# Third attention with its biased rows kept from the first load, and the first feed-forward with base on VectorE and its variance moved up

## The reference, cut to what matters

```python
def head(W, b):
    e = jnp.einsum('bmc,hc->bmh', x, W) + b
    q, k, v = jnp.split(e, 3, axis=1)
    attn = jax.nn.softmax(jnp.einsum('bmd,bnd->bmn', q, k) * SCALE, axis=-1)
    return jnp.einsum('bmn,bnd->bmd', attn, v)
outs = jax.vmap(head)(W_embed, b_embed)
qkv = jnp.concatenate([outs[i] for i in range(outs.shape[0])], axis=1)
out = jnp.einsum('bmd,cd->bmc', qkv, W_out) + b_out
return out + x        # x is _layernorm(h); the caller adds h
```

## Time and profile before

| | us |
|---|---|
| median of the runs shown | 4401.44 |
| the profiled execution | 4401.72 |
| its span | 4399.9 |
| first feed-forward, from its first sum to its last output add | 632.9 to 853.0 |
| third attention, from its first centering to its last output add | 2120.3 to 2409.4 |
| busy over the span: PE, VectorE, ScalarE, GpSimd | 3833.5, 2827.1, 2353.6, 1993.0 |

### The profile page before, as it was taken

One profiled execution on the slowest core, in us unless ns is written; L12 is line 12 of the kernel. 1 busy time (PEld: TensorE's weight loads), 2 busy tenths in 40 slices (PEclk: granted clock), 3 DMA queues, 4 the chain that ended last, 5 costly groups with the idle time before them and its releaser, 6 DMA issues.

```text
span 4399.9 us, 111398 instructions
## 1 busy us (share of the span) xinstructions
PE 3833.5 (87%) x31697; PEld 2615.2 (59%) x31697; DVE 2827.1 (64%) x9320; ACT 2353.6 (53%) x5933; POOL 1993.0 (45%) x2308
## 2 busy tenths in 40 slices
PE   7488857698999799999776769999999999899999
PEld 7355533386666566666665546666666666555555
DVE  2577735585788644444444778888888888455554
ACT  5455524322444344444333547888888888555555
POOL 0144327674666412222454655555555555434333
PEclk9999966697999899999655779999999999899999
DMA  2111123331111333333111220000000000233332
GB/s 53 36 31 31 27 39 100 82 83 41 38 38 36 72 75 77 77 77 79 38 42 44 65 61 10 11 11 11 11 11 11 11 13 17 63 77 76 77 77 56
DMA packets 483268, 207.06 MB, mean 47 GB/s; under 512 B 452850, under 2 KB 473326, under 8 KB 482930
## 3 DMA queue, kind: packets, MB, share of 16 engines
q1 hardware_dynamic: 483058, 204.73, 20.5%
HBM read 158.75 MB, written 45.91 MB: 47 GB/s over the span
## 4 chain that ended last, share of the span: by engine, by line
PE 48%; issue 19%; POOL 15%; DVE 8%; SPq 6%; DMA 2%; ACT 1%; POOLq 0%; DVEq 0%; ACTq 0%
POOL att_P L3588 8%; PE sw_pH L4192 5%; PE moe_pH L2727 5%; PE sw_pY L4179 4%; PE moe_pY L2750 4%; PE att_pS L982 3%; DVE att_M L1177 3%; PE moe_pH L2731 2%; PE moe_pH L2737 2%; POOL att_norm_rstd L673 1%; SPq L2894 1%; PE att_pS L2220 1%; PE att_pO L1044 1%; SPq L2888 1%; PE ret_pR L1837 1%
## 5 line engine op out<-in xcount | busy, mean ns | idle before, releaser
L3588 POOL TENSOR_TENSOR att_P<-att_P,att_rden 125x498 f32<-125x498 f32 x512 | 520.4, 1017 | 510.2 <-DVE att_rden L3883 509.6
L3776 ACT ACTIVATE att_P<-att_Z,att_nb 125x249 f32<-125x249 f32 x1024 | 504.1, 497 | 22.8 <-DVE att_nb L3895 21.3
L2792 DVE TENSOR_TENSOR moe_hT<-moe_silu,moe_pH 128x498 f32<-128x498 f32 x384 | 258.8, 674 | 310.5 <-ACT moe_silu L2776 310.5
L4240 ACT ACTIVATE sw_hT<-sw_pH,sw_b 128x498 f32<-128x498 f32 x512 | 319.0, 675 | 219.7 <-PE sw_pH L4192 219.7
L3697 PEld LDWEIGHTS att_pP<-att_ident,att_P 124*125 124x125 f32 (+1 forms) x2048 | 262.5, 187 | 234.0 <-issue 234.0
L3697 PE MATMUL att_pP<-att_ident,att_P 124*125 124x124 f32 (+1 forms) x2048 | 349.6, 293 | 50.6 <-issue 28.8
L3895 DVE CUSTOM_DVE_ANT_0 att_Z<-att_pS,att_mask 125x249 f32<-125x249 f32 x1024 | 365.8, 412 | 29.3 <-PE att_pS L3685 27.3
L2776 ACT ACTIVATE moe_silu<-moe_pH 128x498 f32<-128x498 f32 x384 | 225.5, 587 | 261.6 <-PE moe_pH L2731 175.9
L3783 ACT ACTIVATE att_PTr<-att_pP 125x498 f32<-125x498 f32 x512 | 297.5, 581 | 100.0 <-PE att_pP L3697 90.9
L2703 POOL TENSOR_TENSOR moe_xe<-moe_share,moe_x 128x1992 f32<-128x1992 f32 x32 | 130.0, 4063 | 428.4 <-DMA moe_share<-mixing 402.1
L4099 POOL TENSOR_TENSOR sw_acc<-sw_acc,sw_Z 128x249 f32<-128x249 f32 x224 | 154.1, 688 | 364.6 <-DVE sw_Z L4319 363.9
(11 more groups left out here) (463 smaller groups left out, 9691.9 us busy)
## 6 DMA issues: line engine op xcount, KB each, us to landing
moe_share<-mixing SPq DMA_DIRECT2D x64, 498.0 KB, 6.1
sw_share<-mixing SPq DMA_DIRECT2D x64, 498.0 KB, 6.1
ffn_W<-in_ffn_pairs SPq DMA_DIRECT2D x64, 192.0 KB, 2.4
att_F<-h_stream SPq DMA_DIRECT2D x192, 62.5 KB
att_X<-h_stream SPq DMA_DIRECT2D x192, 62.5 KB
h_stream<-att_H SPq DMA_DIRECT2D x64, 62.5 KB
ffn_F<-h_stream SPq DMA_DIRECT2D x64, 62.5 KB
ret_F<-h_stream SPq DMA_DIRECT2D x64, 62.5 KB
```

Source lines behind the costliest of these rows:

```text
L3588: g.tensor_tensor(own, own, bc(rden[:, j % 2, c, :], T), ALU.mult).then_inc(*scaled.one())
L3776: ins = a.activation(P[:, r, c, t, :], Z[:, r, c, t, :], ACT.Exp, scale=-1.0, bias=nb[:, r, c, t:t + 1], accum_out=den[:, r, c, t:t + 1])
L4240: a.activation(hT[:, k % 4, :, :], pH[:, place, :, 0:T], ACT.Relu, bias=b1[:, k:k + 1]).then_inc(*hid_ready.one())
```

## The change

**Third attention.** `keep`, X and its semaphore go: SP's loop now issues `ahead` for pair n+6 and `store` for pair n. The add with bias moves from the pair's fifth part to its second, right behind centering, reads F and writes base, which now has six buffers; it waits for the output add of the pair six before. `ahead` waits for this add instead of for centering. Everything that had two buffers keeps two (u % 2), and the loop body has six slots.

**First feed-forward.** base moves from GpSimd's step 2 to VectorE's step 2, behind the product with gamma; VectorE's product with rstd now also waits for the output add of earlier pairs. The tail's variance moves from VectorE's step 3 to step 2, so that it stands ahead of acc and H1.

```diff
--- stage_ffn0, GpSimd
             def last(n, u, step):
                 if step == 0:
                     g.wait_ge(*t_variance.after(n))
                     g.tensor_tensor(trstd[:, :], tvar[:, :], norm.expo[:, :], ALU.pow).then_inc(*t_powered.one())
-                if step == 2:
-                    g.wait_ge(*h_ready.before(n))
-                    g.tensor_tensor(base[:, :, :], g4(Fi[:, u, :, :, :]), bcm(beta[:, :], 1, 4),
-                                    ALU.add).then_inc(*base_ready.one())
--- stage_ffn0, VectorE
             def ends(n, u, step):
-                if step == 3:
+                if step == 2:
                     v.wait_ge(*t_squared.after(n))
...
             def last(n, u, step):
                 if step == 1:
                     v.wait_ge(*t_powered.after(n))
+                    v.wait_ge(*h_ready.before(n))
...
                 if step == 2:
...
+                    v.tensor_tensor(base[:, :, :], g4(Fi[:, u, :, :, :]), bcm(beta[:, :], 1, 4),
+                                    ALU.add).then_inc(*base_ready.one())
--- stage_attention2
-    STEPS, WAVES, ROUNDS = 5, 8, 8
+    STEPS, PERIOD, WAVES, ROUNDS = 5, 6, 14, 8
...
-        X = st.sb("X", [TH, 2, HEADS, 2, C])
...
-        base = st.sb("base", [TH, 2, HEADS, 2, C])
+        base = st.sb("base", [TH, PERIOD, HEADS, 2, C])
...
         def ahead(sp, n, u):
-            sp.wait_ge(*norm.centered.lagging(n))
+            sp.wait_ge(*biased.lagging(n))
...
-        def keep(sp, n, u):
-            sp.wait_ge(*base_ready.lagging(n))
-            st.held(sp)
-            for j, r, src in parts(h, n):
-                sp.dma_start(X[r, u, j, :, :], src).then_inc(*kept.one(u))
...
                     n = j * 2 + u
-                    keep(sp, n + 2, u)
                     ahead(sp, n + 6, u)
                     store(sp, n, u)
             for n in range(PAIRS - 6, PAIRS - 2):
-                keep(sp, n + 2, n % 2)
                 store(sp, n, n % 2)
--- stage_attention2, GpSimd
             def even(n, u, step):
                 if step == 3:
                     g.wait_ge(*xn_ready.before(n))
-                    norm.center(g, n, g4(F[:, u, :, :, :]))
+                    norm.center(g, n, g4(F[:, u % 2, :, :, :]))
+                    if since(n, PERIOD):
+                        g.wait_ge(*h_ready.after(n - PERIOD))
+                        st.held(g)
+                    g.tensor_tensor(base[:, u, :, :, :], F[:, u % 2, :, :, :], bias[:, :, :, :], ALU.add).then_inc(
+                        *biased.one())
...
             def soft(n, u, step):
                 own = base[:, u, :, :, :]
                 if step == 0:
-                    if since(n, 2):
-                        g.wait_ge(*h_ready.after(n - 2))
-                    g.wait_ge(*kept.after(n, u))
-                    g.tensor_tensor(own, X[:, u, :, :, :], bias[:, :, :, :], ALU.add).then_inc(*biased.one())
-                if step == 1:
                     g.wait_ge(*biased.after(n))
                     g.wait_ge(*xn_ready.after(n))
-                    g.tensor_tensor(own, own, xn[:, u, :, :, :], ALU.add).then_inc(*base_ready.one())
-            waves(g, (nothing, even, turn_in, nothing, soft, nothing), STEPS)
+                    g.tensor_tensor(own, own, xn[:, u % 2, :, :, :], ALU.add).then_inc(*base_ready.one())
+            waves(g, (nothing, even, turn_in, nothing, soft, nothing), STEPS, PERIOD)
```

More of the change, by code:

```diff
@@ L2908, in _ @@
                 ahead(sp, n, n)
-                keep(sp, n, n)
         yield
@@ L2950, in turn_in @@
                         g.wait_ge(*xT_done.after(n - 2))
-                    norm.scale(g, n, g4(xn[:, u, :, :, :])).then_inc(*xn_ready.one())
+                    norm.scale(g, n, g4(xn[:, u % 2, :, :, :])).then_inc(*xn_ready.one())
             def soft(n, u, step):
@@ L3011, in proj @@
                     for hd in range(HEADS):
-                        ins = pe.matmul(pA[:, hd * TH:(hd + 1) * TH], G[:, hd, :], xT[:, u, 0:TH], start=True,
+                        ins = pe.matmul(pA[:, hd * TH:(hd + 1) * TH], G[:, hd, :], xT[:, u % 2, 0:TH], start=True,
                                         stop=True)
@@ L3018, in proj @@
                         r = slice(b * C, (b + 1) * C)
-                        ins = pe.matmul(pV[:, b, 0:HEADS * C], xT[r, u, 2 * TH:T], wv[r, :], start=True, stop=True)
+                        ins = pe.matmul(pV[:, b, 0:HEADS * C], xT[r, u % 2, 2 * TH:T], wv[r, :], start=True, stop=True)
                     ins.then_inc(*v_done.one())
@@ L3029, in soft @@
                             r = slice(b * C, (b + 1) * C)
-                            ins = pe.matmul(pS[:, b, hd * TH:(hd + 1) * TH], AT[r, u, hd, :],
-                                            xT[r, u, TH:2 * TH], start=True, stop=True)
+                            ins = pe.matmul(pS[:, b, hd * TH:(hd + 1) * TH], AT[r, u % 2, hd, :],
+                                            xT[r, u % 2, TH:2 * TH], start=True, stop=True)
                     ins.then_inc(*s_done.one())
@@ L3051, in ends @@
                             ins = pe.matmul(pO[:, at:at + C], PTr[:, g * TH:(g + 1) * TH],
-                                            V[:, u, b, hd * C:(hd + 1) * C], start=True, stop=True)
+                                            V[:, u % 2, b, hd * C:(hd + 1) * C], start=True, stop=True)
                     ins.then_inc(*o_done.one())
-            waves(pe, (nothing, nothing, turn_in, proj, soft, ends), STEPS)
+            waves(pe, (nothing, nothing, turn_in, proj, soft, ends), STEPS, PERIOD)
         @block.scalar
@@ L3068, in turn_in @@
                     a.wait_ge(*xT_done.after(n))
-                    a.activation(xT[:, u, :], pX[:, 0:T], ACT.Copy).then_inc(*xT_ready.one())
+                    a.activation(xT[:, u % 2, :], pX[:, 0:T], ACT.Copy).then_inc(*xT_ready.one())
             def proj(n, u, step):
@@ L3075, in proj @@
                         a.wait_ge(*o_done.after(n - 2))
-                    a.activation(V[:, u, :, :], pV[:, :, 0:HEADS * C], ACT.Copy).then_inc(*v_ready.one())
+                    a.activation(V[:, u % 2, :, :], pV[:, :, 0:HEADS * C], ACT.Copy).then_inc(*v_ready.one())
             def soft(n, u, step):
@@ L3086, in soft @@
                             g = b * HEADS + hd
-                            ins = a.activation(P[:, u, g, :], pS[:, b, hd * TH:(hd + 1) * TH], ACT.Exp,
-                                               bias=nb[:, g:g + 1], accum_out=den[:, u, hd, b:b + 1])
+                            ins = a.activation(P[:, u % 2, g, :], pS[:, b, hd * TH:(hd + 1) * TH], ACT.Exp,
+                                               bias=nb[:, g:g + 1], accum_out=den[:, u % 2, hd, b:b + 1])
                     ins.then_inc(*exp_ready.one())
-            waves(a, (nothing, even, turn_in, proj, soft, nothing), STEPS)
+            waves(a, (nothing, even, turn_in, proj, soft, nothing), STEPS, PERIOD)
         @block.vector
@@ L3114, in pre @@
                 if step == 4:
-                    v.wait_ge(*loaded.after(n, u))
+                    v.wait_ge(*loaded.after(n, u % 2))
                     v.wait_ge(*norm.centered.before(n))
-                    norm.sums(v, n, g4(F[:, u, :, :, :]))
+                    norm.sums(v, n, g4(F[:, u % 2, :, :, :]))
             def turn_in(n, u, step):
@@ L3143, in ends @@
                     v.wait_ge(*o_ready.before(n))
-                    v.reciprocal(rden[:, :], den[:, u, :, :].rearrange("p n b -> p (n b)")).then_inc(
+                    v.reciprocal(rden[:, :], den[:, u % 2, :, :].rearrange("p n b -> p (n b)")).then_inc(
                         *den_ready.one())
@@ L3153, in ends @@
                     v.wait_ge(*base_ready.after(n))
-                    v.wait_ge(*stored.lagging(n, u))
+                    v.wait_ge(*stored.lagging(n, u % 2))
                     st.held(v)
-                    v.tensor_tensor(g4(H1[:, u, :, :, :]), tmp[:, :, :], g4(base[:, u, :, :, :]),
+                    v.tensor_tensor(g4(H1[:, u % 2, :, :, :]), tmp[:, :, :], g4(base[:, u, :, :, :]),
                                     ALU.add).then_inc(*h_ready.one())
-            waves(v, (pre, nothing, turn_in, proj, soft, ends), STEPS)
+            waves(v, (pre, nothing, turn_in, proj, soft, ends), STEPS, PERIOD)
         yield
```

7 lines of the change are left out of this document (3 added, 4 removed).

## The result

The changed kernel took 4319.44 us in the median of four runs (4316.81 to 4323.29), the kernel before 4401.63 beside it (4396.05 to 4402.95): a ratio of 0.9821, 95% interval 0.9809 to 0.9833. The forecast was 4323, with a range of 4302 to 4354. The two profiled executions differ by 84.9 us of span.

A forecast was written before the change was run, and what follows sets the result against it. SP's issue was taken to bound the third attention, a ring of GpSimd and VectorE the first feed-forward. Terms -61.8 + 0.8 - 17.8 = -78.8 us from 4401.7 gave 4323 us, range 4302 to 4354.

The forecast's parts named there:

- SP's issue sets the slot before: Third attention: SP's three groups of six issues cost 9.04 us a slot; without second loads, about 6.2.
- PE comes next at 6.57, at a clock of 0.50: Third attention: with nothing late, PE takes 6.57 us per pair at the 1.2 GHz level, the slot's lower end.
- the first rival: Third attention: PE gets its full 2.4 GHz clock, SP's 6.2 a slot bounds, 76.7 us gained, 4308 us; chance 0.08.
- the ring over two slots of 13.52: Third attention: chain from scores' transposes through VectorE and ScalarE to the next, 6.76 us a slot; 6.75 taken, 61.8 us gained.
- The first add moved, 0.8 us in the filling slots: Third attention: the moved add frees its buffer 0.99 us later, delaying loads once while filling: 0.8 us lost (0 to 1.5).
- Six slots a loop body, nothing: Third attention: four loop passes instead of thirteen; fewer returns gain nothing, or up to 3 us, left out.
- rival 4: Third attention: returns of the larger loop body wait for code, making the kernel slower, 4443 us at 40 us each; chance 0.02.
- First feed-forward, 5.9 a slot: First feed-forward: slot falls from 6.56 to 5.9 us, between two PE and ScalarE values, 5.66 and 6.05: 17.8 us gained.
- the ring from centering over the squares and the variance to `acc` and the coming variance: First feed-forward: longer ring through VectorE and GpSimd, 4.9 us with hand-offs, up to 6.1 with delayed tiny scalings.
- Base on VectorE at 0.43, in a gap: First feed-forward: base takes about 0.43 us on VectorE where it waits for the tail's squares; GpSimd loses 0.74 of 5.44.
- the second rival: Both stages: VectorE and GpSimd lock each other out, 7.8 and 7.3 us a slot, 4389 us; chance 0.03 at full size.
- Variance ahead, the wait of 1.13 goes: First feed-forward: tail's variance no longer behind the output add, so power follows centering and GpSimd's 1.13 us wait goes.

The follow-up runs named there:

- e_sp6: The changed kernel with the six second loads per pair issued by SP again, into a buffer nobody reads or waits for: 4378.4 us.
- e_sp1: The changed kernel with the second load's bytes per pair moved in one DMA on SP, read by nobody: 4330.3 us.
- e_pe: The changed kernel with two of three heads' matmuls into pA left out in the third attention's loop: 4313.8 us, one run.
- e_att: The kernel before with only the third attention's part of the change, first feed-forward as before: 4355.8 us, ratio 0.9903.
- e_base: The kernel before with only the feed-forward's base add moved to VectorE, tail's variance left behind the output add: 4361.5 us, ratio 0.9922.
- e_pad: The kernel before with the third attention's part of the change and 17 one-column memsets on VectorE at that stage's head: 4340.5 us, ratio 0.9864.
- again_best: The changed kernel with the tail's variance left behind the output add, repeat timing on one chip with the change: 4312.8 us, ratio 0.9794.
- e_first: The changed kernel with the tail's variance left behind the output add and base put ahead of VectorE's two scalings: 4307.6 us, ratio 0.9787.
- again_after: The changed kernel itself, timed once more: 4319.8 us, ratio 0.9818.

## Why the prediction held, and where it didn't

- **SP's issue sets the slot before**: right, shown by `e_sp6` and `e_sp1`. The estimate was that 12 issues cost 6.2 a slot; they cost 6.32 in `e_pe`.
- **PE comes next at 6.57, at a clock of 0.50**: right; 17 of 27 slots are at that floor, and the first rival, the full clock once PE's pauses are gone, didn't come: 0.50 with PE busy for 99.7% of 170 us. The step that failed is the ring over two slots of 13.52, from which 6.75 was taken. VectorE's output add did get slower, as feared (0.92 us in the mean between 2130 and 2320, before 0.74 between 2160 and 2390), but PE hardly ever waits for that chain, and `e_pe` runs at 6.32 with the same VectorE and GpSimd work (though less of PE's, of which the ring holds a part), so in the change the ring doesn't set the slot. It was read in a stretch in which PE itself was full, and so probably counted waits for PE as work of the ring. Mis-sized by 27 x 0.11 = 3 us. The full slots gave 244.06 - 179.28 = 64.8 us; some 2.4 of them were lost at the stage's head (last section), so the stage as a whole gained 62.5.
- **The first add moved, 0.8 us in the filling slots**: not seen. First to fifth transposes took 23.29 us before and 23.23 after. Its own cost was hidden.
- **Six slots a loop body, nothing**: right in that stage. But the changed program moved another stage's loop, a cost that no step of the prediction had: rival 4 looked for a wait for code at the returns of the changed loop, and VectorE's pauses came in a stage behind, 25.2 us in `e_att`. In the change they are 14 of 0.44 us, and the fourth attention took 1163.0 us instead of 1158.7. That they are waits for code is argued, not shown.
- **First feed-forward, 5.9 a slot**: the gain was under-sized (26.8 us instead of 17.8), and the step behind the number is the one that failed. The 5.9 was taken between two values of a path through PE and ScalarE, 5.66 and 6.05. In the change that path doesn't set the slot, which is 5.60 at a high clock and 5.66 at the low one. The clock of the stage also rose, from 0.64 to 0.73 (windows, 660 to 820), so the long hidden-layer groups of 2.03 were not the rule. What holds is the ring from centering over the squares and the variance to `acc` and the coming variance. The prediction had it, at 4.9 to 6.1, but as the shorter one. PE does come in where the variance is last: at the low clock `e_base` takes 5.87.
- **Base on VectorE at 0.43, in a gap**: wrong where GpSimd works on whole rows, 0.83 (27 of 32 pairs in the change); right beside its powers, 0.42 (31 of 32 at most 0.42 in `e_base`). The rule weighed in the prediction, that the two engines lock each other out (the Trainium skill, SBUF — State Buffer, Who interferes with whom), agrees with the first. It doesn't give the second by itself, as the power reads SBUF too, four values a row. And the 0.69 that the prediction put beside the rule is a scaling with one tensor as input, not two. Full-size locks, the second rival, didn't come.
- **Variance ahead, the wait of 1.13 goes**: it went, and moved to the power of the coming pair as predicted (17.0 us, 27 times, from 660 to 820). With base alone it goes only where PE's clock is high (0.14 in the good slots, some 0.9 to 1.1 in most of the long ones), and yet `e_base` is faster in the mean. The prediction took both edits as one gain. It listed what stands behind the variance in its new place, but not that `acc` need not wait for the squares if the variance stays where it was.
- **Tail slots at nothing**: 26.8 us in the stage, of which 27 x 0.97 = 26.2 are full slots. Right.

## What to carry to other kernels

Count a queue's issues per turn of the loop before looking at its waits: here six DMAs that nobody needed to wait for cost as much as six that somebody did. Before moving an instruction ahead on an engine whose order the program fixes, list what then stands behind its input; the edit that shortens one ring can lengthen the next. When a stage's clock varies, sort its slots by clock before comparing two orders: here one order is better at the high clock and the other at the low. And compare stages, not only totals: a gain in one stage can hide or be hidden by a shift in code that nobody changed.

## What had not been expected of the hardware

- Seventeen idle instructions on VectorE took 24.5 us from a stretch with a loop of 14 passes in a later stage (`e_att`, `e_pad`). Another order in an earlier stage took 4.6 us from the same loop (`again_best`, `e_first`).
- PE's clock can differ at the same place between two executions of the same kernel. While PE folds the weights at the head of the third attention, it was granted 0.51 in the first profile of the change (windows; columns as above):

```profile
2085.00:2087.00 2.00, 1.76 (x29) 1.68 (x29) 0.57 (x3) 0.00 (x0) 0.00 (x0) 1.00 0.19 41
2087.00:2093.00 6.00, 5.98 (x57) 5.65 (x56) 0.00 (x0) 0.00 (x0) 0.00 (x0) 0.51 0.05 10
```

  and 1.00 in that of `again_after`:

```profile
2086.00:2092.00 6.00, 4.98 (x82) 4.66 (x80) 0.92 (x5) 0.00 (x0) 0.00 (x0) 1.00 0.11 24
```

  In the six profiles with the low clock there (0.50 to 0.54) the stage's first transposes came 15.0 to 15.4 us after the last `moe` store, in the eight others 12.6 to 12.8. So differences of 2.5 us between single profiles of this stage mean nothing.
